# Attention heads in pairs: two scores back to back, then the two mixings one pair behind

## What is computed

```
x = rmsnorm(tokens) ; q, k, v = x @ Wq, x @ Wkv ; q, k = l2norm(q)*scale, l2norm(k)*scale
sim  = tanh(q k^T / 50) * 50 / 8, causal
out  = softmax(sim) @ v
h    = layernorm(tokens + out @ Wout)
```

## Time and profile before

| | us |
|---|---|
| median of 3 runs (lowest, highest) | 2177.25 (2175.13, 2180.91) |
| span of the profiled execution | 2164.7 |
| busy in it: TensorE | 1900.8 (88%) |
| busy: VectorE, ScalarE, GpSimd | 1211.3, 855.2, 770.5 |

### The profile page before, as it was taken

The page is one execution under the profiler, slowest core; times in us unless marked ns, Lnnn a source line. Parts: engine busy times, 40 slices in busy tenths (PEclk is TensorE's granted clock), DMA queues, the critical chain, the costliest instruction groups (busy, mean ns, idle before and its releaser), DMA issues. The chain is left out here.

```text
span 2164.7 us, 31212 instructions
## 1 busy us (share of the span) xinstructions
PE 1900.8 (88%) x11768; PEld 1639.7 (76%) x11768; DVE 1211.3 (56%) x1671; ACT 855.2 (40%) x1164; POOL 770.5 (36%) x505
## 2 busy tenths in 40 slices
PE   4789999998927998998998899959999999999997
PEld 4788888888926786777777777748787877877876
DVE  7999999899933655557465555632413314134141
ACT  5553443455124564466465545612222212222121
POOL 3222222123143543445354334514333333243332
PEclk9899999999958989999997899979999999999999
DMA  9122212112021000200110010033000000000000
GB/s 144 71 91 77 110 45 91 72 45 118 1 88 53 21 14 8 80 14 21 51 37 21 7 53 21 21 128 128 20 1 19 19 0 19 0 19 20 1 10 11
DMA packets 32211, 95.87 MB, mean 44 GB/s; under 512 B 18630, under 2 KB 18758, under 8 KB 26569
## 3 DMA queue, kind: packets, MB, share of 16 engines
q1 hardware_dynamic: 31500, 89.80, 13.0%
q10 hardware_dynamic: 576, 4.19, 0.5%
HBM read 81.37 MB, written 24.15 MB: 49 GB/s over the span
## 5 line engine op out<-in xcount | busy, mean ns | idle before, releaser
L445 PE MATMUL conv<-w_hi,x_hi 128*128 128x368 f16 (+5 forms) x1320 | 358.8, 281 | 8.8 <-POOL w_lo L191 4.6
L445 PE MATMUL conv<-w_lo,x_hi 128*128 128x368 f16 (+5 forms) x1320 | 359.2, 281 | 0.0
L445 PE MATMUL conv<-w_hi,x_lo 128*128 128x368 f16 (+5 forms) x1320 | 357.5, 280 | 0.0
L760 POOL TENSOR_TENSOR probs<-probs,mask 128x512 f32<-128x512 f32 x128 | 178.5, 1400 | 281.8 <-ACT probs L841 281.7
L1042 PE MATMUL mixed<-v,probs 128*128 128x65 f32 x1536 | 226.6, 304 | 22.5 <-POOL probs L760 14.6
L1042 PEld LDWEIGHTS mixed<-v,probs 128*128 128x128 f32 x1536 | 210.1, 217 | 39.4 <-POOL probs L760 16.1
L1216 POOL TENSOR_TENSOR ha_lo<-raw_c,ha_hi 128x512 fp32r<-128x512 f32 x128 | 164.9, 1288 | 209.5 <-DVE ha_hi L1266 209.5
L1254 ACT ACTIVATE raw_c<-ring,sh 128x512 f32<-128x512 f32 x128 | 88.1, 688 | 372.6 <-PE ring L1351 372.5
L1351 PE MATMUL ring<-ha_hi,wh 128*128 128x512 f32 x512 | 208.9, 408 | 16.9 <-POOL ha_lo L1216 16.9
L1351 PE MATMUL ring<-ha_lo,wh 128*128 128x512 f32 x512 | 206.7, 404 | 0.0
L445 PEld LDWEIGHTS conv<-w_hi,x_hi 128*128 128x128 f16 x1320 | 193.0, 146 | 17.4 <-issue 9.6
(11 more groups left out here) (141 smaller groups left out, 3907.1 us busy)
## 6 DMA issues: line engine op xcount, KB each, us to landing
xt<-x_columns_in SPq DMA_DIRECT2D x12, 1163.0 KB, 5.1
xp<-x_patches_in SPq DMA_DIRECT2D x12, 1152.0 KB, 5.1
hidden_words<-hidden_weights_in SPq DMA_DIRECT2D x8, 1408.0 KB, 9.1
words<-hidden_words SPq DMA_DIRECT2D x32, 352.0 KB, 3.1
wh<-hidden_words SPq DMA_DIRECT2D x2, 4096.0 KB, 21.2
tokens<-result ACTq DMA_DIRECT2D x4, 1024.0 KB, 3.9
hn<-tokens SPq DMA_DIRECT2D x4, 1024.0 KB, 5.4
h<-tokens SPq DMA_DIRECT2D x4, 1024.0 KB, 7.5
```

Source lines behind the costliest of these rows:

```text
L445: ins = pe.matmul(out, xs[:, c, RI - 1 - i:RI - 1 - i + NR, :, x].rearrange("p r g -> p (r g)"), w, start=(t == 0), stop=(t == len(terms) ...
L760: pool.tensor_tensor(diag, diag, both, ALU.mult).then_inc(s_mask, 1)
```

## The change

`attention_order` now walks over heads in pairs (n, n + 1). Inside an image the two scores stand first, then mix n - 2, the slot of head n, mix n - 1, the slot of head n + 1. Where a new image begins, both mixes of the pair come first, then both scores, then both slots. The transposes of the outputs, the `rms` steps and the `bits` steps come after the pair in which they stood. Nothing else is touched; every wait in the engines' code is by the same counts as before. The part of the list for heads 20 to 26 of a BODY group:

```diff
--- before.py
+++ after.py
@@ -503,28 +503,35 @@
 def attention_order(last):
 
     order = []
-    for n in range(NH + 2):
-        img, hd = n // HEADS, n % HEADS
-        now = [("score", n)] if n < NH else []
-        if n >= 2:
-            now.append(("mix", n - 2))
-        order += reversed(now) if hd == 0 else now
-        if img < GI - 1:
-            order += [(kind, img + 1, k) for kind, k in SLOTS[hd]]
-        elif not last and img == GI - 1 and hd == 0:
-            order += [("turn_h", k) for k in range(2, 4)]
-        elif not last:
-
-            slot = {NH: None, NH + 1: len(SLOTS) - 1}.get(n, hd - 1)
-            order += [(kind, GI, k) for kind, k in SLOTS[slot]] if slot is not None else []
-        if n >= 2 and (n - 2) % HEADS == HEADS - 1:
+    for n in range(0, NH + 2, 2):
+        pair = (n, n + 1)
+        scores = [("score", k) for k in pair if k < NH]
+        mixes = [[("mix", k - 2)] if k >= 2 else [] for k in pair]
+        if n % HEADS == 0:
+            order += mixes[0] + mixes[1] + scores
+            mixes = [[], []]
+        else:
+            order += scores
+        for k, mix in zip(pair, mixes):
+            img, hd = k // HEADS, k % HEADS
+            order += mix
+            if img < GI - 1:
+                order += [(kind, img + 1, x) for kind, x in SLOTS[hd]]
+            elif not last and img == GI - 1 and hd == 0:
+                order += [("turn_h", x) for x in range(2, 4)]
+            elif not last:
+
+                slot = {NH: None, NH + 1: len(SLOTS) - 1}.get(k, hd - 1)
+                order += [(kind, GI, x) for kind, x in SLOTS[slot]] if slot is not None else []
+        if n >= 2 and (n - 1) % HEADS == HEADS - 1:
             order += [("turn_o", (n - 2) // HEADS, b) for b in range(2)]
-        if not last and n == NH - HEADS - 1:
-            order += [("turn_h", k) for k in range(2)]
-        if not last:
-            order += {RMS_AT: [("rms_sum", 0)], RMS_AT + 2: [("rms_root", 0)], RMS_AT + 4: [("rms_scale", 0)]}.get(n, [])
-        if n % (NH // CHUNKS) == 2 and n < NH:
-            order.append(("bits", n // (NH // CHUNKS)))
+        for k in pair:
+            if not last and k == NH - HEADS - 1:
+                order += [("turn_h", x) for x in range(2)]
+            if not last:
+                order += {RMS_AT: [("rms_sum", 0)], RMS_AT + 2: [("rms_root", 0)], RMS_AT + 4: [("rms_scale", 0)]}.get(k, [])
+            if k % (NH // CHUNKS) == 2 and k < NH:
+                order.append(("bits", k // (NH // CHUNKS)))
     return order + [("project", k) for k in range(4)]
```

## The result

The changed kernel takes 2200.5 us (median of 4 runs, 2196.75 to 2207.61), against 2176.27 before (2175.13 to 2180.91): a ratio of 1.013, 95% interval 1.0094 to 1.0167. It is slower by 24 us; 2196 was predicted. The profiled execution's span is 2195.0, against 2164.7.

What follows compares the result with a forecast made beforehand. TensorE was taken as the bound of the attention stage (busy 676 of 757 us), leaving its idle and low-clock time to change. Terms -4 + 4 + 0 - 2 + 17 + 4 = +19 gave span 2184, time 2196; range 2170 to 2213.

Steps and rivals of the forecast that it cites:

- The fourth image: Fourth images of three groups: first projection job starts 5.6 us later, waiting on ht_lo; +17 us with clock loss.
- T8's new wait: Second images: the first transposing job newly waits 2.2 us for keys, their scale taking 4.6 us beside two masks.
- Second images: Heads 8 to 15 scored: low clock expected again, +1 us for each of four images, +4 in all.
- the 1.5 us priced for X14 and X15: Second images: the low clock starts 1.5 us later, so mixings of heads 14 and 15 lose about 1.5 us.
- Third images: Heads 16 to 23: norm's root and scaling hold mixings 20 and 21 in both orders; 0, bounds -3 and +3 each.
- First and last images: First images -2 us in all; last image of the last group +4, bounds +2 and +9.
- the 12.5 us "for what lies around the span": Median of 2177.25 less profiled span of 2164.7, added to the span forecast of 2184 to give 2196.
- (a): Faster: the clock stays up in second and third images, -10 us in all, 2167; chance 0.16.
- (b): No change: fourth image costs only its ScalarE part, cancelled by the pairs' gain; 2177 us; chance 0.17.
- (c): Much slower: waits of every second mixing and of transposing jobs lower the clock; 2213 us, at most 2230; chance 0.13.

Runs made afterwards that it cites:

- the experiment on it: Changed kernel with the old single order for the last image of the last group: 2194.36 us, ratio 1.0086.
- k6: Changed kernel with GpSimd's mask cut to the first column of each diagonal block, most of the causal mask left out: 2122.58 us, ratio 0.9758.
- the three together: Changed kernel with single order in pairs that start an image and in the last image, and RMS_AT 13 instead of 17: 2137.15 us, ratio 0.9818.
- k9: Changed kernel, complete, with GpSimd's masks between a root and its scale held back until after the scale, in both chains: 2209.58 us, ratio 1.0164.

## Why the prediction was right, point by point

**The fourth image: right, and the main term.** I had M0 wait 4.9 us for ht_lo behind two tanh-exp pairs and X23 2.6 for VectorE. The changed kernel's TensorE, ScalarE and VectorE there, to be laid beside the earlier trace rows:

```profile
1010.84 1.52 PE L1049 MATMUL mixed<-v,probs 128*128 128x65 f32 x12 [2.31 <-DVE parts L926]
...
1019.84 0.79 PE L1011 MATMUL job<-wqkv_hi,ht_hi 128*128 128x512 f32 x1 [3.36 <-DVE ht_lo L895]
```

```profile
1014.93 0.79 ACT L845 ACTIVATE probs<-sim 128x768 f32<-128x768 f32 x1
1015.76 0.84 ACT L848 ACTIVATE probs<-probs 128x768 f32<-128x768 f32 x1
1016.51 2.07 ACT L811 ACTIVATE ht_hi<-job 128x512 fp32r<-128x512 f32 x2
```

```profile
1017.65 2.14 DVE L895 TENSOR_TENSOR ht_lo<-job,ht_hi 128x512 fp32r<-128x512 f32 x2 [4.28 <-ACT ht_hi L811]
```

ht_hi follows exp 25 without a gap, as in the walk. In the other two groups the wait is 4.9 us; here the low clock had already stretched the H steps, and 3.4 are left. From X22 to M0 the three images take 12.7 us each instead of 7.3: 5.4 more, where 5.6 were walked. The whole term was +17 and measured 21.5. The 4.5 us too few lie behind M0, and most of them are the clock's: 17 to 20 us of each of these images are at the low level, 10 to 17 before, where I had priced 1 us each. Some 1.7 us are idle time: T12 now waits 1.75 us in each, instead of 0.31 to 2.57, and T8 3.9 instead of 3.2, which the walk had not reached.

**T8's new wait: right in its mechanism.** 2.2 us were predicted. The scale of chain 0 with two masks beside it, and T8:

```profile
934.21 2.30 DVE L907 TENSOR_TENSOR raw<-raw,rn 128x1024 f32<-128x1024 f32 x1 [2.54 <-POOL rn L761]
936.44 2.35 DVE L909 TENSOR_TENSOR keys<-raw,rn 128x512 f32<-128x512 f32 x2
```

```profile
938.84 0.65 PE L1023 MATMUL job<-ident_b,raw 128*128 128x128 f32 x4 [2.58 <-DVE keys L909]
```

4.6 us, as assumed, and T8 waits 2.58 where it waited for nothing in the earlier trace rows; in all eight second and third images it is 2.56 to 2.62. X7 waits 1.10 for the read of X6, much as predicted (1.0).

**Second images: the sum was wrong, by the clock.** I expected the low clock behind T12 in each of them, as before, and 1 us lost. In groups 1 and 3 the clock fell at T8 already, the array was then late enough to find T12's keys ready within 0.3 us, and the image took 40.9. In groups 2 and 4 T12 waits 2.60, the clock fell there, and the image took 42.7 to 42.8; but this low stretch lasts 6.8 us where that of before lasts 10.2, so the 1.5 us priced for X14 and X15 did not come. One wait paid for the other. 3.1 us were won where 4 were to be lost.

**Third images: the term that failed.** I had written that the norm's root and its scaling "hold X20 and X21 in both orders" and taken 0, with bounds of 3 each way; it was +14.7. The fourth group, which has no norm, shows whose it is: its third image lost 1.3 us, the other three 13.3. In the old order X20 did wait for its mask behind the norm's root, but X21 did not wait for VectorE, since S23 stands between T12 and X21. TensorE and VectorE of before in group 2:

```profile
989.09 2.82 PE L1042 MATMUL mixed<-v,probs 128*128 128x65 f32 x12 [3.66 <-POOL probs L760]
...
994.28 1.63 PE L1042 MATMUL mixed<-v,probs 128*128 128x65 f32 x12
```

```profile
987.85 5.20 DVE L881 TENSOR_SCALAR hn<-hn,rms 128x256 f32<-128x256 f32 x8 [0.93 <-POOL rms L740]
```

Paired, S23 is spent before X20, and two waits follow each other with only four transposes between. The rows of VectorE and TensorE of the changed kernel in group 2:

```profile
994.17 6.21 DVE L888 TENSOR_SCALAR hn<-hn,rms 128x256 f32<-128x256 f32 x8 [0.93 <-POOL rms L747]
```

```profile
995.42 2.37 PE L1049 MATMUL mixed<-v,probs 128*128 128x65 f32 x12 [2.98 <-POOL probs L767]
...
1001.08 2.79 PE L1049 MATMUL mixed<-v,probs 128*128 128x65 f32 x12 [2.43 <-DVE parts L926]
```

X21 waits 2.43 us for a read that stands behind 6.2 us of scaling, with the clock already down; in groups 1 and 3 it waits 3.65. The scaling starts 36.0 us after X14 instead of 32.0. So the step that failed is the overlap "in both orders": the wait of X21 is new. Moving the norm took 8.5 to 9.4 us off each of these images; the same move in the kernel before was worth 3 us in the three together. I should have walked this image as I walked the second.

**First and last images.** The first won 6.9 us, not 2, although T8's wait grew by 0.4 to 1.2 us and not by 0.3 at most; 4.5 of them are group 1's, where the low clock takes 3.4 us instead of 13.9. The last lost 6.8, not 4, and the experiment on it gave 6 back.

**The sum.** +19 was predicted; +30.3 came between the profiled spans, +24 in the medians. The direction and the largest term were sound. That the total came out close is in part luck. The failed third term (+15) was offset by the first and second images (-12 against their terms). And the 12.5 us "for what lies around the span" are no such thing: 1.7 to 1.8 lie around it, and the rest is that the profiled execution of the kernel before was 10 us faster than its median. The span forecast of 2184 was therefore missed by 11 us, the time of 2196 by 4.5.

**The rivals.** (a), the clock stays up, did not happen: 191 us of the stage are at the low level, 164 before, and in five of the eight second and third images the clock is low behind T12. The row of the last image, from S24 and S25 to the first transposes of its output:

```profile
1415.20:1446.00 30.80, 25.56 (x169) 22.98 (x168) 11.18 (x29) 14.48 (x18) 10.16 (x8) 0.73 0.05 16
```

No wait in it is over 0.83 us (X23's, just ahead of it, is 1.10), and its mean clock is 0.73. The Trainium skill, page "TensorE: Matmul & The Clock Gate", section "Why this matters for your kernels", warns of long gaps; this row shows that thin work with short ones is enough. (b) is out by the fourth image's 21.5 us. (c), 2213 and more, was not reached.

## What to carry to other kernels

When steps of several engines follow one list, a reordering is priced by walking each distinct stretch of that list, chain by chain, and not one of them as a pattern: here one pair in sixteen and one norm made most of the loss, while the same idea inside an image was worth about 1.6%, with the norm moved 1.8% and with the masks of chain 0 held back 2.3%. Count for each chain what cover stands between its start and its reader, and what is let go on the neighbouring engine at the moment when it runs. A wait removed ahead of a second chain can mostly move, as it did here, and the clock can add to it or take from it; test combinations, since single edits gave less (or lost) where the sum won.

## What was not expected of the hardware

- Beside two masks of 1.28 us the scale took 4.6 us instead of 2.4, beside one 3.5. What that costs in time is not shown by the 78 us that k6 won, since k6 leaves the masks' work out: with the masks held back the changed kernel won nothing, and the three together 15 us. The Trainium skill, page "SBUF — State Buffer", section "Terms", has the two engines exclude each other for a whole instruction; k6 and k9 agree in kind; the length of 4.6 is 0.4 under the 5.0 that this rule would give, by an estimate from 2.4 and two masks of 1.28.
- A gain can be taken back through the clock: moving the norm won 8.5 us in one image and cost 4.9 in the next, with no new wait there, its mean clock falling from 0.87 to 0.79.
- Matmuls whose results are overwritten, 66.7 us of them, cut the time at the low clock from 191 to 124 us and made the kernel 19 us faster by the medians.
